# Layer norms by halves of four tiles: ScalarE writes the first half's rows, VectorE measures and writes the second's, TensorE turns tile by tile

## What is computed

```python
def _layernorm(x, axis=-1, eps=1e-05):
    m = jnp.mean(x, axis=axis, keepdims=True)
    v = jnp.var(x, axis=axis, keepdims=True)
    return (x - m) / jnp.sqrt(v + eps)
...
    x = x + _L0_xattn_ref(_layernorm(x, axis=-1), ctx_1024, ctx_1024, L0_xattn_w_q, L0_xattn_w_k, L0_xattn_w_v, L0_xattn_w_o)
...
    x = x + _L3_ffn_ref(_layernorm(x, axis=-1), L3_ffn_weight_q, L3_ffn_weight_scale, L3_ffn_bias)
```

## Time and profile before

| | |
|---|---|
| median of 3 runs | 4200.3 us (4199.68 to 4204.29) |
| the profiled execution's own time | 4197.01 us |
| its span in the trace | 4195.2 us |
| mean granted TensorE clock | 0.924 |
| TensorE (PE) busy | 3610.4 us (86%) |
| weight loads (PEld) busy | 2577.3 us (61%) |
| VectorE (DVE) busy | 2145.2 us (51%) |
| ScalarE (ACT) busy | 1644.0 us (39%) |
| GpSimd (POOL) busy | 688.9 us (16%) |

### The profile page before, as it was taken

The page is one execution under the profiler, slowest core; times in us unless marked ns, Lnnn a source line. Parts: engine busy times, 40 slices in busy tenths (PEclk is TensorE's granted clock), DMA queues, the critical chain, the costliest instruction groups (busy, mean ns, idle before and its releaser), DMA issues. The chain is left out here.

```text
span 4195.2 us, 91339 instructions
## 1 busy us (share of the span) xinstructions
PE 3610.4 (86%) x39376; PEld 2577.3 (61%) x39376; DVE 2145.2 (51%) x4277; ACT 1644.0 (39%) x2972; POOL 688.9 (16%) x338
## 2 busy tenths in 40 slices
PE   6999999689887979999768888899999698998975
PEld 4666666566655667778534445677777585554554
DVE  5666666645553367766534445455655423333335
ACT  4667676221221177776323333344444111111212
POOL 1667667000000000000211010111010000000001
PEclk9999999899998999999768889999999868999987
DMA  2001010100111315540010000211110002220610
GB/s 72 34 33 49 34 42 25 50 26 10 35 35 55 134 49 183 181 148 12 14 44 0 0 0 0 78 52 45 43 52 19 21 1 89 96 86 11 227 35 14
DMA packets 156718, 224.18 MB, mean 53 GB/s; under 512 B 39863, under 2 KB 136051, under 8 KB 156220
## 3 DMA queue, kind: packets, MB, share of 16 engines
q1 hardware_dynamic: 156348, 218.73, 15.8%
HBM read 217.65 MB, written 1.05 MB: 52 GB/s over the span
## 5 line engine op out<-in xcount | busy, mean ns | idle before, releaser
L2781 POOL TENSOR_TENSOR x_sc<-x_sc,h_T 128x2048 f32<-128x2048 f32 (+1 forms) x105 | 442.4, 4246 | 248.4 <-ACT h_T L2989 248.4
L2601 ACT ACTIVATE x_sc<-x_sc,x_nb 128x2048 f32<-128x2048 f32 (+1 forms) x112 | 210.6, 1880 | 297.6 <-DVE x_sc L2650 297.4
L3064 DVE TENSOR_TENSOR x_most<-x_most,ps 128x512 f32<-128x512 f32 (+1 forms) x352 | 234.8, 685 | 81.8 <-PE ps L2897 69.7
L2650 DVE SCALAR_TENSOR_TENSOR x_sc<-ps,x_nb,x_cap 128x2048 f32<-128x2048 f32 (+1 forms) x112 | 246.2, 2198 | 49.9 <-PE ps L2542 49.9
L1550 ACT ACTIVATE s1i_both<-ps,s_less,s_rs_s 128x64 f32<-128x64 f32 x624 | 213.7, 425 | 71.0 <-DVE s_less L1656 70.8
L2968 ACT COPY x_sc<-ps 128x1024 f32<-128x1024 f32 x192 | 179.3, 944 | 133.4 <-PE ps L2897 85.9
L2854 PE MATMUL ps<-x_wv,x_ctx_T 128*128 128x256 f32 (+1 forms) x832 | 205.0, 388 | 0.0
L2982 ACT ACTIVATE x_sc<-x_sc 128x2048 f32<-128x2048 f32 (+1 forms) x112 | 201.1, 1797 | 4.0 <-DVE x_sc L2781 4.0
L2513 PE MATMUL ps<-x_ctx_T,x_wk 128*128 128x401 f32 (+1 forms) x512 | 200.0, 517 | 1.5 <-PEq L44 1.5
L2846 PE MATMUL ps<-x_ctx_T,x_wk 128*128 128x401 f32 (+1 forms) x512 | 194.8, 518 | 3.6 <-POOL x_v L2810 3.4
L2521 PE MATMUL ps<-x_wv,x_ctx_T 128*128 128x256 f32 (+1 forms) x832 | 197.7, 379 | 0.0
(11 more groups left out here) (520 smaller groups left out, 7212.1 us busy)
## 6 DMA issues: line engine op xcount, KB each, us to landing
x_ctx_T<-in_ctx_T SPq DMA_DIRECT2D x32, 1601.0 KB
s1i_ctx_T<-in_ctx_T SPq DMA_DIRECT2D x16, 1601.0 KB, 7.2
x3i_ctx_T<-in_ctx_T SPq DMA_DIRECT2D x16, 1601.0 KB, 6.6
s1i_ctx_n<-in_ctx SPq DMA_DIRECT2D x16, 1536.0 KB
x3i_ctx_n<-in_ctx SPq DMA_DIRECT2D x16, 768.0 KB
h<-in_ctx SPq DMA_DIRECT2D x12, 896.0 KB
e_w<-in_L_attn_W SPq DMA_DIRECT2D x8, 1024.0 KB
rows<-in_ctx SPq DMA_DIRECT2D x12, 640.0 KB
```

The source lines that it names most:

```text
L2601: nc.scalar.activation(x, x, ACT.Square, scale=DH ** -0.5, bias=nb[0:keys, 0:1]).then_inc(squared, 1)
L2650: nc.vector.scalar_tensor_tensor(out=slot[0:keys].rearrange("p r m h j q -> p (r m h) (j q)")[:, :, 0:width], in0=score_banks[0:keys].rear ...
L2781: return eng.tensor_tensor(x, x, most_of, ALU.subtract)
L3064: ins = nc.vector.tensor_tensor(best[0:keys, rs], best[0:keys, rs], score_banks[0:keys, rs, :, j, :], ALU.max)
```

## The change

The norm is split into two halves of four tiles. VectorE measures and folds the first four tiles, measures the fifth, inverts the first half's deviations and computes a new small tile `shift` = -mean * rstd (128 x 4) for them. ScalarE writes the first four tiles as `rstd * x + shift`, with the second half's square root between its third and fourth tile. Meanwhile VectorE measures the other three tiles, folds, inverts, and writes the second four tiles as before. TensorE now goes tile by tile: it waits for one tile and turns both of its channel halves. Two semaphores (`rows_act`, `rows_dve`) take the place of `rows_ready`, `shift_ready` is new, `early` is gone: ten semaphores where nine were. The unused `affine` and `early` paths are taken out.

```diff
             @block.vector
             def _(dve):
                 steps = Steps(dve, own)
-                for t in range(T):
-                    steps.done(nc.vector.bn_stats(env.bn[:, t, :], src[:, t, :]))
-                steps.wait()
-                for t in range(T):
-                    nc.vector.bn_aggr(env.mv[:, t, :], env.bn[:, t, :]).then_inc(stats, 1)
-
-                dve.wait_ge(std_ready, 1)
-                steps.done(nc.vector.reciprocal(env.rstd[:, :], env.std[:, :]))
-                steps.wait()
-                for t in range(T):
+                def measure(tiles):
+                    for t in tiles:
+                        steps.done(nc.vector.bn_stats(env.bn[:, t, :], src[:, t, :]))
+                def aggregate(half):
+                    steps.wait()
+                    for t in range(HALF * half, HALF * (half + 1)):
+                        nc.vector.bn_aggr(env.mv[:, t, :], env.bn[:, t, :]).then_inc(stats, 1)
+                def invert(half):
+                    ts = slice(HALF * half, HALF * (half + 1))
+                    dve.wait_ge(std_ready, half + 1)
+                    steps.done(nc.vector.reciprocal(env.rstd[:, ts], env.std[:, ts]))
+                    steps.wait()
+                measure(range(HALF))
+                aggregate(0)
+                measure(range(HALF, HALF + 1))
+                invert(0)
+                nc.vector.scalar_tensor_tensor(
+                    out=env.shift[:, :], in0=env.mv[:, 0:HALF, 0], scalar=-1.0,
+                    in1=env.rstd[:, 0:HALF], op0=ALU.mult, op1=ALU.mult).then_inc(shift_ready, 1)
+                measure(range(HALF + 1, T))
+                aggregate(1)
+                invert(1)
+                for t in range(HALF, T):
                     nc.vector.tensor_scalar(nat[:, t, :], src[:, t, :], env.mv[:, t, 0:1],
                                             env.rstd[:, t:t + 1], ALU.subtract,
-                                            ALU.mult).then_inc(rows_ready, 1)
+                                            ALU.mult).then_inc(rows_dve, 1)
...
             @block.scalar
             def _(act):
-                act.wait_ge(stats, T)
-                nc.scalar.activation(env.std[:, :], env.mv[:, :, 1], ACT.Sqrt,
-                                     bias=env.eps5[:, 0:1]).then_inc(std_ready, 1)
+                def deviations(half):
+                    ts = slice(HALF * half, HALF * (half + 1))
+                    act.wait_ge(stats, HALF * (half + 1))
+                    nc.scalar.activation(env.std[:, ts], env.mv[:, ts, 1], ACT.Sqrt,
+                                         bias=env.eps5[:, 0:1]).then_inc(std_ready, 1)
+                deviations(0)
+                act.wait_ge(shift_ready, 1)
+                for t in range(HALF):
+                    if t == HALF - 1:
+                        deviations(1)
+                    nc.scalar.activation(nat[:, t, :], src[:, t, :], ACT.Identity,
+                                         scale=env.rstd[:, t:t + 1], bias=env.shift[:, t:t + 1]
+                                         ).then_inc(rows_act, 1)
...
             @block.tensor
             def _(pe):
-                for half in range(2 if dst_T is not None else 0):
-                    pe.wait_ge(rows_ready, 4 * half + 4)
+                for t in range(T if dst_T is not None else 0):
+                    half, at = t // HALF, t % HALF * P
+                    if half == 0:
+                        pe.wait_ge(rows_act, t + 1)
+                    else:
+                        pe.wait_ge(rows_dve, t - HALF + 1)
                     for f in range(KT):
-                        for t in range(4):
-                            last = nc.tensor.transpose(
-                                env.ps[:, 2 * half + f, t * P:(t + 1) * P],
-                                nat[:, 4 * half + t, f * P:(f + 1) * P], env.ident)
-                        last.then_inc(turned, 1)
+                        last = nc.tensor.transpose(env.ps[:, 2 * half + f, at:at + P],
+                                                   nat[:, t, f * P:(f + 1) * P], env.ident)
+                        if t % HALF == HALF - 1:
+                            last.then_inc(turned, 1)
```

More of the change, by code:

```diff
@@ L79, in wview, with layernorm @@
     return ap.rearrange("(k p) n -> p k n", p=P)
-def layernorm(nc, env, stage, src, nat, dst_T, affine=None, early=(), loads=()):
-    with signals(nc, stage, "loaded early own stats std rows turned act_out dve_out") as (
-            loaded, affine_in, own, stats, std_ready, rows_ready, turned, act_out, dve_out):
+def layernorm(nc, env, stage, src, nat, dst_T, loads=()):
+    HALF = T // 2
+    with signals(nc, stage, "loaded own stats std shift_ready rows_act rows_dve turned act_out "
+                 "dve_out") as (
+            loaded, own, stats, std_ready, shift_ready, rows_act, rows_dve, turned, act_out,
+            dve_out):
         with nc.Block() as block:
@@ L91, in _ @@
             def _(sp):
-                load_all(sp, early, affine_in)
                 load_all(sp, loads, loaded)
@@ L108, in _ @@
                     nc.vector.tensor_scalar(nat[:, t, :], src[:, t, :], env.mv[:, t, 0:1],
                                             env.rstd[:, t:t + 1], ALU.subtract,
-                                            ALU.mult).then_inc(rows_ready, 1)
-                if early:
-                    dve.wait_ge(affine_in, 16 * len(early))
+                                            ALU.mult).then_inc(rows_dve, 1)
                 for half in range(2 if dst_T is not None else 0):
                     dve.wait_ge(turned, 2 * half + 2)
[L115 to L120, removed]
+                    nc.vector.tensor_copy(dst_T[:, 1, half * NH:(half + 1) * NH],
+                                          env.ps[:, 2 * half + 1, :]).then_inc(dve_out, 1)
@@ L122, in _ @@
             @block.scalar
             def _(act):
-                act.wait_ge(stats, T)
-                nc.scalar.activation(env.std[:, :], env.mv[:, :, 1], ACT.Sqrt,
-                                     bias=env.eps5[:, 0:1]).then_inc(std_ready, 1)
-                if early:
-                    act.wait_ge(affine_in, 16 * len(early))
+                def deviations(half):
[3 more added lines that the diff above has]
+                                         bias=env.eps5[:, 0:1]).then_inc(std_ready, 1)
@@ L130, in _ @@
                     act.wait_ge(turned, 2 * half + 1)
-                    out, put = dst_T[:, 0, half * NH:(half + 1) * NH], env.ps[:, 2 * half, :]
-                    if affine is None:
-                        nc.scalar.copy(out, put).then_inc(act_out, 1)
-                    else:
-                        nc.scalar.activation(out, put, ACT.Identity, scale=affine[0][:, 0:1],
-                                             bias=affine[1][:, 0:1]).then_inc(act_out, 1)
+                    nc.scalar.copy(dst_T[:, 0, half * NH:(half + 1) * NH],
+                                   env.ps[:, 2 * half, :]).then_inc(act_out, 1)
@@ L3987, in build @@
         env.std, env.rstd = sb("std", [P, T]), sb("rstd", [P, T])
+        env.shift = sb("shift", [P, T // 2])
         consts = sb("consts", [P, d["consts"].shape[1]])
```

## The result

| | before | changed |
|---|---|---|
| median | 4203.4 us (4198.9 to 4213.5, 12 runs) | 4191.9 us (4185.2 to 4197.1, 12 runs) |
| profiled execution | 4197.0 us | 4189.1 us |
| its span | 4195.2 us | 4187.3 us |
| mean granted clock | 0.924 | 0.925 |
| SP's waits at the norms' barriers, 13 in all | 48.5 us | 38.5 us |

The runs of before in the first column were taken beside those of the changed kernel. The ratio is **0.9969, interval 0.9959 to 0.9978**, which is 13.0 us less (9.2 to 17.2). The medians lie 11.5 apart; the ratio weighs every run and not the middle ones alone. Forecast were 4189.7 us, a range of 4183 to 4197, and a saving of 10.6 us.

The account below looks back on a forecast made before the run. Each norm is bound by its own chain of steps, VectorE alone and then TensorE. 5 x 1.85 + 2 x 0.70 = 10.65, say 10.6 us, off the median of 4200.3 gives 4189.7 us, range 4183 to 4197.

Parts of the forecast that it names:

- The chain: Inside a norm: end at 7.99 instead of 9.84, 1.85 us less where tiles are turned, 0.70 less where not.
- Which calls gain: From SP's waits: the seven calls whose compute was last gain; the six whose loads end last give 0.
- a change in the load-bound calls: Sign of being wrong: calls that were bound by loads become shorter or longer than before; 0 was forecast there.
- What is late next: In every turning norm after the change, TensorE at clock 0.50 is late next.
- I take no net change: TensorE's clock behind the five unbound turning norms: partly chance, so counted as no net change.
- e0_in: One of the six norm calls whose loads end last: SP's second wait is 0.2 us, gain forecast 0.
- 1 (the clock turns against it): Gaps between transpose pairs make s1 and x3 come out cold: saving 4.9, 4195.4 us; chance 0.17.
- 2 (the clock turns for it): Behind the norms f0, a1 and f2 come out warm: 6.35 us more, saving 17, 4183.3 us; chance 0.12.
- 3: A table load holds up the first square root in the norm; chance 0.04.
- 4: ScalarE's rows cost near 0.69 us: saving 7.5, 4192.8 us; at 1.2 us slower, 4207.5 us; chance 0.06.
- 5: ScalarE's second root comes late, so the first half's turning slides onto the second's: saving 4.9, 4195.4 us; chance 0.03.

Follow-up runs that it names:

- the seven alone: Changed kernel with the new norm only in the seven calls whose compute ends last, the old norm in the other six: 4191.4 us, ratio 0.9963.
- the six alone: Changed kernel with the new norm only in the six calls whose loads end last, the old norm in the other seven: 4209.4 us, ratio 1.0007.

## Why the prediction was right

**The chain.** Right to 0.05 us in s1 at every step that the end hangs on; only ScalarE's third row ended 0.10 late, and its tile's transposes came 0.09 late, which hardly moved the end. The sum was 10.6 and the blocks measure 10.2. The gap is x3 (1.49 in place of 1.85), under whose last transposes the clock already rose in before, and the ScalarE row, which took 0.03 to 0.04 more than line 1297 had said, less 0.12 us that the clock gave back inside `f2_ln`.

**Which calls gain.** Right: the seven alone give 0.9963 and the six alone 1.0007. I had named a change in the load-bound calls as a sign against me, and they did become 1.8 us shorter. But `a2_ln` does so with the old norm too, and two profiles of before differ by 1.1 us there, so it is the scatter of the loads. The barrier wait of SP picked the seven, though its change is not exact in the smallest case (q3: 0.4 less for a block 0.68 shorter, so 2.0 left where 1.7 was predicted).

**What is late next.** TensorE at clock 0.50, as said: the eight transposes of the second half and VectorE's copy follow each other without a gap in s1. Warming it shortened the norm by 0.82.

**The clock: "I take no net change".** This term was put at nothing, and it probably is not nothing, though small. The chain gives 10.2 us. That lies inside the interval of the first comparison (9.2 to 17.2 us) and of the seven alone (10.1 to 21.5), and outside that of the changed kernel's second series (0.9959, 11.4 to 23.1). An estimate from all three series with the seven new norms: the means differ by 13.2, 14.3 and 16.1 us, together 14.5 with some 2 us either way, so about 4 us more than the chain. In the same direction, the 96 runs of before beside the experiments have a mean clock of 0.9214 and those of the three series 0.9240, 0.9225 and 0.9243. In the traces TensorE's clock falls or stays behind `f0_ln` and `x3_ln`: these stretches are 3.7 and 3.6 us shorter on average in the three traces of those series than in the six with longer norms. But the e0_in, a1 and a3 stretches move by 2 to 3 us as well, not all in the same direction, and six against three traces are too few to add them up. I looked for the surplus in the wrong place, the first 3 to 6 us after a norm: those did not improve (cold busy time behind the norms, counted as above, was 41.0 us before and 38.8 and 42.5 after). At f0 the difference arises later, at the narrow matmuls.

How much of the surplus is the f0 stretch is not settled, because one profile shows one execution only. That the first pair of profiles shows 7.9 us and the medians 11.5 has one reason in the first profile of before, which had both the short f0 stretch and the short a3 stretch (119.9, where twelve of the fourteen traces have 126.0 to 128.1).

**The number.** That 4191.9 came so near to 4189.7 is in part luck. The forecast was taken off a median of three runs, 4200.3, which was 3.1 us lower than that of the twelve beside the changed kernel, and the saving was forecast lower than it came out; the two errors offset each other.

**The rivals.** 1 (the clock turns against it): s1 did come out cold, x3 did not, and s1's stretch was 2.5 us longer in this pair of profiles. In the changed kernel's second profile s1 came out cold again, and its stretch was as long as before (551.3), so this cold start has no price that can be seen. 2 (the clock turns for it): f0, a1 and f2 stayed cold (0.50, 0.50 and 0.51), so what it counted on did not happen; what the clock gave back, it gave elsewhere. Both rivals count a cold stretch at half its length; in s1 ten transposes took 2.40 us at 0.50 and 1.58 at 1.00, so there it was a third. 3, that a table load holds up the first root, falls: in s1 the load ends at 1458.70, the folds at 1459.27 and the root starts at 1459.31, 1.86 after the first statistics. It comes right behind the folds, and no trace shows a delay behind a load: in the earlier trace rows, where a root stands right behind one, it starts 0.02 us after the load's end. Both traces execute the same number of table loads, 111. 4 falls: rows cost 0.586 although both engines read `x` and write `h` at once. 5 falls: the second root begins at 4.09, between the third row and the fourth, where it belongs, and all seven gained.

## What to carry to other kernels

Where blocks stand between barriers, sum the chain inside one block from its own rows, and read from SP's second wait which calls can turn a shorter chain into time; both can be had to a few hundredths of a microsecond before anything is run. Splitting work between engines and handing it over in small pieces paid together more than apart here (1.80 against 0.97 and 0.53 us), since each needs the other. But where a saving is 0.2% and TensorE is busy for 86% of the time, the level of its clock in single stretches moves by as much: stretches of the same code differed by 4 to 8 us between traces, and runs of the same kernel by up to 36 us. So compare stretches of equal code in several traces, and don't judge such a change by one total.

## What the runs showed of the hardware

- ScalarE's Identity with a scale and a bias of one value per partition, 128 x 256 from SBUF, takes 0.586 us and 0.50 from start to start; with a fixed scale it is 0.417.
- 32 matmuls of 8 columns keep TensorE busy for all of 4.30 us, and the clock can fall under them all the same (0.80 in that window, 0.58 in the next). It did in five traces of fourteen, in which it had risen 0.6 to 0.8 us ahead of them; in the nine in which it had risen 1.1 to 1.8 us ahead it stayed at 1.00.
- The same stretch of code can take one of two lengths: 127.1 to 127.7 or 131.5 to 131.6 us behind f0, 361.4 to 362.5 or 366.0 to 366.2 behind f2. Behind x3 it takes lengths in between as well (176.2 to 181.1), and they go with the cold time in it.
- Times of one kernel go with its mean granted clock: before took 4197.0 at 0.924 and 4219.4 at 0.916. Its 96 runs beside the experiments span 4189.2 to 4225.4 us, at 0.926 and 0.914.
